# Two granules of the rotation behind each of the last three convolution steps

## The reference

```python
x = x + depthwise_conv5x5(gn(x), kernel(weight))       # each channel with its own 5x5 taps
x = x + einsum('hvc,bchw->bvhw', R, gn(x))             # for each image row h a 128x128 matrix R[h]
```

## Time and profile before

| | us |
|---|---|
| median of 3 runs | 428.61 (428.4 to 429.36) |
| the profiled execution | 428.04 |
| its span | 426.2 |
| PE busy | 407.3 (96% of the span) |
| DVE busy | 362.2 (85%) |
| ACT busy | 264.4 (62%) |
| POOL busy | 242.6 (57%) |
| bytes moved by DMA | 139.83 MB (10^6), mean 328 GB/s |

### The profile page before, as it was taken

One profiled execution on the slowest core, in us unless ns is written; L12 is line 12 of the kernel. 1 busy time (PEld: TensorE's weight loads), 2 busy tenths in 40 slices (PEclk: granted clock), 3 DMA queues, 4 the chain that ended last, 5 costly groups with the idle time before them and its releaser, 6 DMA issues.

```text
span 426.2 us, 8616 instructions
## 1 busy us (share of the span) xinstructions
PE 407.3 (96%) x3110; PEld 200.7 (47%) x3110; DVE 362.2 (85%) x691; ACT 264.4 (62%) x513; POOL 242.6 (57%) x312
## 2 busy tenths in 40 slices
PE   7899999999999999999999999999999994999992
PEld 2345555555555555544444445444444541444440
DVE  4899999999999999889998889999887783687872
ACT  2386676667656775696666777666677534477760
POOL 7588675667656765696555676555553153344440
PEclk9999999999999999999999999999999998899997
DMA  8826579599977677977899999999999999999998
GB/s 295 374 58 226 213 221 316 220 334 380 373 250 281 241 272 270 341 255 245 339 360 372 301 384 344 352 391 330 411 361 394 407 377 386 401 427 427 424 425 344
DMA packets 36955, 139.83 MB, mean 328 GB/s; under 512 B 7472, under 2 KB 7600, under 8 KB 24368
## 3 DMA queue, kind: packets, MB, share of 16 engines
q1 hardware_dynamic: 17056, 107.29, 66.5%
q10 hardware_dynamic: 19856, 31.99, 20.8%
HBM read 72.14 MB, written 67.12 MB: 327 GB/s over the span
## 4 chain that ended last, share of the span: by engine, by line
PE 89%; POOL 3%; DMA 2%; issue 2%; DVE 1%; ACT 1%; ACTq 0%; SPq 0%; POOLq 0%
PE ps L743 61%; PE ps L778 26%; POOL area L447 2%; PE ps L784 2%; DMA kept<-x_scratch 1%; DMA norm<-affine 1%; DVE area L652 1%; PE ps L753 1%; PE ps L761 0%; ACT gn L542 0%; POOL gn L470 0%; POOL area L461 0%; ACTq L261 0%; DVE tin L652 0%; ACT std L514 0%
## 5 line engine op out<-in xcount | busy, mean ns | idle before, releaser
L743 PE MATMUL ps<-area 64*64 64x496 f32 (+2 forms) x2560 | 281.6, 586 | 2.4 <-POOL area L447 2.4
L743 PEld LDWEIGHTS ps<-area 64*64 64x64 f32 x2560 | 140.3, 133 | 98.4 <-issue 86.4
L447 POOL TENSOR_TENSOR area<-mask,area 128x325 f32<-128x325 f32 x128 | 132.3, 1056 | 44.3 <-PE ps L743 33.0
L778 PE MATMUL ps<-gn,rot 128*128 128x512 f32 x256 | 117.3, 611 | 6.2 <-ACT gn L542 5.9
L521 ACT ACTIVATE area<-area,affine 128x256 f32<-128x256 f32 x192 | 97.9, 588 | 34.4 <-DVE affine L632 32.5
L534 ACT ACTIVATE area<-ps 64x512 f32<-64x512 f32 x128 | 75.6, 591 | 31.2 <-PE ps L743 28.5
L610 DVE BATCH_NORM_STATS2 stats<-area 128x6 f32<-128x512 f32 x128 | 80.6, 689 | 3.8 <-DMA area<-in_x_dram 3.8
L778 PEld LDWEIGHTS ps<-gn,rot 128*128 128x128 f32 x256 | 48.3, 194 | 72.3 <-issue 60.4
L461 POOL TENSOR_SCALAR area<-area,affine 128x256 f32<-128x256 f32 x62 | 46.1, 752 | 63.3 <-DVE affine L632 63.2
L619 DVE BATCH_NORM_STATS2 stats<-area 128x6 f32<-128x512 f32 x128 | 81.1, 697 | 1.1
L652 DVE TENSOR_TENSOR tin<-ps,tin 128x512 f32<-128x512 f32 x68 | 46.8, 691 | 15.7 <-PE ps L778 15.6
(11 more groups left out here) (26 smaller groups left out, 110.3 us busy)
## 6 DMA issues: line engine op xcount, KB each, us to landing
area<-in_x_dram SPq DMA_DIRECT2D x31, 1024.0 KB, 6.5
x_scratch<-area ACTq DMA_DIRECT2D x29, 1024.0 KB, 7.4
out_dram<-tin SPq DMA_DIRECT2D x17, 1024.0 KB, 8.9
tin<-x_scratch SPq DMA_DIRECT2D x15, 1024.0 KB, 11.4
out_dram<-area SPq DMA_DIRECT2D x10, 1024.0 KB, 13.2
area<-x_scratch SPq DMA_DIRECT2D x7, 1024.0 KB, 11.8
rot<-in_rota_dram SPq DMA_DIRECT2D x4, 1024.0 KB, 9.1
kept<-x_scratch SPq DMA_DIRECT2D x16, 256.0 KB, 10.2
```

Of the source, the lines that this page charges most:

```text
L447: last = nc.gpsimd.tensor_tensor(taps[k % TRING][:, c * KW:(c + 1) * KW].rearrange("p d (b r) -> p d b r", r=TAPS), mask[:].rearrange("p d ...
L743: last = nc.tensor.matmul(ps[half, bank + c].rearrange("p (j w) -> p j w", j=J)[:, :, outs], taps[k % TRING][rows, (2 * pair + c) * KW + d ...
L778: nc.tensor.matmul(ps[:, rot_bank(m), :], rot[:, n % UNITS * RH + h], gn[n % NRING][:, h], start=True, stop=True).then_inc(rotated, 1)
```

## The change

Behind steps 29, 30 and 31 two granules are rotated in place of one (`granules_of`): 10 and 11, 12 and 13, 14 and 15; for step 31, the first behind its matmuls as before, and granule 15 right after it with the last averages between its rows. Thirteen granules of the first half rotated by the end of step 31 and its rotation become sixteen. ACT and POOL normalise them, and DVE adds them, in the same steps.

In SP's order the loads of the loop's iterations 29, 30 and 31 stay at their places and fetch other granules (12 and 11, 14 and 13, 15, where there were 11 and 13, 12 and 14, 15). Granule 11 is stored in iteration 31 instead of 32, granules 12 and 13 in iteration 32 instead of behind the loop. Quarters 0 to 2 are loaded ahead for nine granules, 20 to 28, where there were six, 20 to 25; granules 26 to 28 were loaded whole, later. `IN_QUARTERS` goes from 10 to 13. The buffers of granules 11 to 31 are dealt out anew, and with them the waits for stored granules: 9, 10 and 11 within the loop, 12 and 13 behind it.

```diff
+TWICE = STEPS_ALL - 3
-IN_QUARTERS = 10
+IN_QUARTERS = 13
...
-        tin = [own[n % DRING] for n in range(KEPT)] + [granule_on(at_x[n]) for n in (2, 3, 4)]
+        tin = [own[n % DRING] for n in range(11)]
+        tin += [granule_on(at_x[2]), own[3], granule_on(at_x[3]), own[0], granule_on(at_x[4])]
         tin += [kept[:, n] for n in range(FRONT)]
-        tin += [own[1], granule_on(at_x[5]), own[2], granule_on(at_n[0]), granule_on(at_n[1]), granule_on(at_t),
-                granule_on(at_t + TILE), granule_on(at_x[0]), own[3], granule_on(at_x[1]), own[0], granule_on(at_x[2])]
+        tin += [own[1], own[2], granule_on(at_x[2]), own[3], granule_on(at_x[3]), granule_on(at_x[5]),
+                granule_on(at_n[0]), granule_on(at_n[1]), granule_on(at_t), granule_on(at_t + TILE),
+                granule_on(at_x[0]), granule_on(at_x[1])]
...
+        def granules_of(s):
+            if s < TWICE:
+                return range(s - START, s - START + 1)
+            first = TWICE - START + 2 * (s - TWICE)
+            return range(first, first + 2)
-        LAST_THREE = KEPT * RH - 1
+        LAST_THREE = granules_of(STEPS_ALL - 1)[0] * RH
```

In SP's loop over s:

```diff
-                    store_granule(sp, s - START - 2)
+                    for n in granules_of(s - 2):
+                        store_granule(sp, n)
...
                     store(sp, s - 2)
-                    store_granule(sp, 11)
+                    for n in granules_of(s - 2):
+                        store_granule(sp, n)
                     load_norms(1)
-                n = s - START + 1
-                if 2 <= n < KEPT:
+                if START + 1 <= s < STEPS_ALL - 1:
+                    n = granules_of(s + 1)[0]
                     if n >= DRING:
-                        sp.wait_ge(out_stored[n - DRING], 16)
+                        sp.wait_ge(out_stored[{12: 7, 14: 8}.get(n, n - DRING)], 16)
                     load_granule(sp, n)
-                n = s - 29 + KEPT
-                if KEPT <= n < UNITS:
+                if s >= TWICE and s < STEPS_ALL:
                     await_stores(sp, s - 3)
                     sp.wait_ge(stats_ready, measured(s - 3 + LAG))
-                    load_granule(sp, n)
+                    load_granule(sp, granules_of(s)[1])
...
-                    for n, left in ((20, 9), (22, 10)):
+                    for n, left in ((20, 9), (21, 10), (22, 11)):
                         sp.wait_ge(out_stored[left], 16)
```

Behind that loop, where afterwards stores 14 and 15 and loads 29 to 31 follow without a wait for a store, and granules 26 to 28 are no longer loaded whole:

```diff
             for r in range(QUARTERS - 1):
-                load_quarter(sp, 21, r)
+                load_quarter(sp, 25, r)
+            for n, left in ((23, 12), (24, 13)):
+                sp.wait_ge(out_stored[left], 16)
+                for r in range(QUARTERS - 1):
+                    load_quarter(sp, n, r)
             sp.wait_ge(convolved, 2 * STEPS_ALL)
             for r in range(QUARTERS - 1):
-                load_quarter(sp, 23, r)
+                load_quarter(sp, 26, r)
             store(sp, STEPS_ALL - 1)
-            for n in (24, 25):
+            for n in (27, 28):
                 for r in range(QUARTERS - 1):
                     load_quarter(sp, n, r)
-            store_granule(sp, 12)
             await_stores(sp, STEPS_ALL - 1)
             for n in range(UNITS, UNITS + IN_QUARTERS):
                 load_quarter(sp, n, QUARTERS - 1)
```

On ACT (POOL normalises in the same order):

```diff
+                if s > TWICE:
+                    normalise_rows(granules_of(s)[0])
                 evict(s, 0)
                 store(act, s - 1)
-                if s + 1 >= START:
+                if START <= s + 1 <= TWICE:
                     normalise_rows(s + 1 - START)
+                if s >= TWICE:
+                    normalise_rows(granules_of(s)[1])
             s = STEPS_ALL - 1
             evict(s - 1, 1)
             take_root(s + 1)
-            normalise_rows(KEPT)
+            normalise_rows(UNITS - 2)
             send_norms(act, s - 3)
             evict(s, 0)
+            normalise_rows(UNITS - 1)
             evict(s, 1)
```

On DVE, and on PE:

```diff
-                add_rows(s - START, range(RH))
+                for n in granules_of(s):
+                    add_rows(n, range(RH))
...
                 if s >= START:
-                    rotate(s - START, range(RH))
+                    for n in granules_of(s):
+                        if n < UNITS - 1:
+                            rotate(n, range(RH))
             last_round = ROUNDS - 1
-            rotate(KEPT, (0, 1))
+            rotate(UNITS - 1, (0, 1))
```

More of the change, by code:

```diff
@@ L50 @@
 START = 19
-KEPT = STEPS_ALL - START
+TWICE = STEPS_ALL - 3
 DRING = 4
@@ L379, in _ @@
                 load_quarter(sp, n, QUARTERS - 1)
[L380 to L385, removed]
             store_granule(sp, 14)
             load_granule(sp, 29)
-            sp.wait_ge(out_stored[12], 16)
+            store_granule(sp, 15)
+            sp.wait_ge(stats_ready, measured(ROUNDS - 1))
             load_granule(sp, 30)
-            store_granule(sp, 15)
-            sp.wait_ge(out_stored[13], 16)
             load_granule(sp, 31)
@@ L496, in _ @@
                     spread_taps(s + 2, (2, 3))
-                if s + 1 >= START:
+                if START <= s + 1 <= TWICE:
                     normalise_rows(s + 1 - START)
-            for n in range(KEPT, GRANULES):
+                if s == TWICE:
+                    normalise_rows(granules_of(s)[1])
+                if s > TWICE:
+                    for n in granules_of(s):
+                        normalise_rows(n)
+            for n in range(granules_of(STEPS_ALL - 1)[0], GRANULES):
                 normalise_rows(n)
@@ L577, in _ @@
             send_norms(act, s - 2)
-            normalise_rows(KEPT + 1)
             take_root(s + 3)
-            normalise_rows(KEPT + 2)
             send_norms(act, s - 1)
             send_norms(act, s)
-            for n in range(KEPT + 3, GRANULES):
+            for n in range(UNITS, GRANULES):
                 normalise_rows(n)
@@ L710, in _ @@
             measure_sum(s)
-            add_rows(KEPT - 1, (0, 1))
+            add_rows(UNITS - 2, (0, 1))
             deviate(s + 3)
-            add_rows(KEPT - 1, (2,))
+            add_rows(UNITS - 2, (2, 3))
             scale(s + 3)
-            add_rows(KEPT - 1, (3,))
-            for n in range(KEPT, GRANULES):
+            for n in range(UNITS - 1, GRANULES):
                 add_rows(n, range(RH))
@@ L819, in _ @@
                 if s >= START:
-                    rotate(s - START, range(RH))
+                    for n in granules_of(s):
+                        if n < UNITS - 1:
+                            rotate(n, range(RH))
             last_round = ROUNDS - 1
-            rotate(KEPT, (0, 1))
+            rotate(UNITS - 1, (0, 1))
             for half in (low, high):
                 average_mean(last_round, half)
-            rotate(KEPT, (2, 3))
+            rotate(UNITS - 1, (2, 3))
             for half in (low, high):
                 average_spread(last_round, half)
-            for n in range(KEPT + 1, GRANULES):
+            for n in range(UNITS, GRANULES):
                 rotate(n, range(RH))
```

## The result

The changed kernel takes 433.55 us (median of 4 runs, 432.74 to 434.56) against 428.99 for the kernel before beside it: a ratio of 1.0107, 95% interval 1.0074 to 1.0140, some 4.6 us slower. The profiled execution took 432.74 with a span of 430.9, against 428.04 and 426.2. It was forecast slower, to 436.9, with a range from 431 to 441.

The account below looks back on a forecast made before the run. PE and the DMA engines were taken as near-equal bounds at the end. Granule 16's last quarter 10.6 us later, less 2.3 from the last landing, gave +8.3 on 426.2, hence median 436.9 us, range 431 to 441.

Parts of the forecast that it names:

- last quarter: Granule 16's last quarter load, which lets PE start again: forecast to land at 367.8, 10.6 us later than 357.2.
- store of 13: Granule 13's store in SP's iteration 32: forecast to land at 353.6, with SP's later quarters and x1 store behind its wait.
- likeliest case: The forecast's main chain to the kernel's end: 436.9 us, own range 434 to 440, chance 0.70.
- lowest bound: Whole kernel at 433.7: store of 13 landing 2.6 us earlier and a last landing of 4.0 instead of 4.6.
- step 3: SP's iteration 32 begins at 340.5; stores land at 348.4, 351.0 and 353.6, SP by then free and waiting.
- lower bound for this store: Store of 13 without a queue at 340.5: landing at 351.0 rather than 353.6, kernel at 434.3.
- 58.2 of rotations: PE's gapless run over granules 16 to 31, slow clock at its start included, kept at 58.2 us after the restart.
- last half store: Final store at the kernel's end: forecast to land in 4.6 us against 6.9 before, returning 2.3 us.
- B: Rival: granule 13's normalising on ACT comes 2.6 us late, so step 31 ends later too; 439.5 us, chance 0.09.
- A: Rival: store of 13 lands by 348, x1 store out at 352, PE 5.1 us later; 431.4 us, chance 0.10.
- C: Rival, not slower: DMA engines set the end, granule 16 in time by 359.5; 426.3 us, chance 0.11.
- Signs: Expected trace: x1 store near 357 after SP waits, PE idling 16 to 17 us, DMA share falling after some 390.

Follow-up runs that it names:

- experiment 1: Changed kernel with the x1 store of step 31 issued first behind SP's loop, ahead of the waits for stores 12 and 13: 434.07 us, ratio to before 1.0125.
- experiment 3: Kernel before, no rotation moved, x1 store of step 31 issued behind the quarters of 24 and 25 and the store of granule 12: 433.11 us, ratio 1.0101.
- experiment 7: Changed kernel with quarters loaded ahead for granules 20 to 25 only, 26 to 28 loaded whole later: 434.96 us, ratio to before 1.0150.
- experiment 5: One unused 0.72 MB transfer added to the tail of both kernels: before 430.56 us, ratio 1.0043; changed 433.16 us, ratio to before 1.0113.
- experiment 2: Changed kernel, x1 store of step 31 first and last quarters of 16 to 23 ahead of the wait for store 13: 430.53 us, ratio to before 1.0044.

## Why the prediction came out right, and what in it was luck

The direction was right, and so was the path: more ahead of x1's last store in SP's order, a later last quarter, a longer idling of PE, part of it returned by the last landing. The link in its middle was not: SP hardly stands at the store of 13. The sum was too large, +8.3 against +4.7 in the profiled executions. The median of 433.55 lies in the range from 431 to 441, but under the likeliest case's own 434 to 440 and just under its lowest bound, 433.7. Three terms each err the same way by 1.2 or 1.3 us: the last quarter, the run of rotations and the last landing.

- *"SP is by then free and waits"*, in step 3, is what failed. SP waited 0.2 us for that store. The sum gave SP nothing for the three loads of norms, 4.03 us, nor for the issues beside them; in the trace it comes to the wait at 351.6, and the store lands at 351.8. That the two fall together is luck, and the forecast of x1's store came near by it. Of the 11.6 us by which the last quarter goes out later, 6.7 are the later start of iteration 32 (7.3 forecast) and 4.9 SP's longer issuing.
- *The store of 13* landed at 351.8, forecast 353.6. The queue was shorter than I counted: iteration 31 began at 323.7 and not 324.4, behind engines that stood part idle, and store 10 landed in 5.8 us, at 329.5, forecast 330.8. The x1 store went out at 355.8 (357.4), landed at 362.3 (363.5), the last quarter at 366.6 (367.8). The times kept their order, 1.2 us early. (The lower bound for this store has a slip: 5.8 and twice 2.6 from 340.5 on give 351.5 and not 351.0, and the bound's time is 434.8. And the row of DMA shares holds 19 slices of nine tenths and a last one of eight, not 18.)
- *The 58.2 of rotations* were taken over whole, with the slow clock in them. Measured 57.0. In the changed kernel the clock granted was 0.50 from the restart at 369.4 to 373.0 and 1.00 behind it:

```profile
369.40:373.00 3.60, 3.59 (x5) 1.52 (x6) 0.69 (x1) 2.42 (x5) 0.71 (x2) 0.50 0.98 380
373.00:376.00 3.00, 3.00 (x8) 1.34 (x7) 2.30 (x4) 0.99 (x2) 0.91 (x2) 1.00 1.00 418
```

  That is 3.6 us at 1.2 GHz, against 6.0 in the kernel before (from its restart at 360.0 to 366); at half speed the 2.4 us fewer are worth 1.2. PE had stood idle longer, and the clock came back sooner, but the one does not follow from the other: after 16.77 us of idling in experiment 1 the same run took 57.65 us, and over all the runs shown here it takes 56.6 to 58.2. This term's miss is chance.
- *The last half store* took 3.3 us, forecast 4.6, because I took a store as unhindered that was not: the 5.8 of 309.6, at a time when the DMA engines were full. The quarter taken as unhindered, 4.3, was not either: while SP waited in experiments 3 and 7, granule 16's last quarter landed in 3.0. The Trainium skill's rule (DMA: Bandwidth & Descriptors, Anatomy of one DMA — SWDGE (gpsimd) path) gave an estimate of 3.2, and the trace agrees with it: 3.3. I had set it aside for a row that measured something else.
- *B* did not occur: the double rotations have no gap. *A* is near in its number, 431.4, but the x1 store did not go out at 352. In experiment 1 the store was early, at 347.5, and the last quarter was not, because what stood between them had not moved. *C* named the right other bound (experiment 5). Its condition, granule 16's last quarter landed by 359.5, was missed by 7 us; experiment 2 came near it, 360.2, and its queue was not emptied: engines that are full to the end give back little for an earlier PE, 1.9 us for 6.4 there.
- *Signs:* the DMA share was to fall after some 390; it fell after 410. The sum had emptied the queue before the stores, but they join it from 375.6 on: a store landed in 15.6 us there and in 7.8 at 403.1, 1 us less from each to the next. "SP waiting for stores" before x1's store was 0.2 us. That x1's store would be the one link that decides was too simple: its place matters (experiment 3), but moving it alone returns nothing (experiment 1).

## What to carry to other kernels

A chain that ended last names what released a wait, not how long anyone stood at it: read the wait itself, and what the waiting engine did before. When two resources are both near their bound, cost an edit on each of them: what it does to the chain of the busiest engine, and how many microseconds the DMA engines go without work. A queue issued in program order, as here, needs, ahead of each wait, enough bytes to last until the wait is over; and steps made longer need more bytes in each. Before taking a row as an unhindered transfer, look at the DMA share in its stretch.

## What the runs showed of the hardware

Idle time of the DMA engines showed in the end of the kernel: 3.0 us of it in two stretches of experiment 3 with 4.1 us more span, 3.2 in experiment 7 with 2.6 us more span, although PE started 2.2 us earlier. And 0.72 MB more in a full queue cost 2.2 us in the median, with an interval from 1.2 to 2.5; 425 GB/s give 1.7. An issue took SP 0.61 us in the six quarters from 351.81 on and 1.34 in the three loads of norms, both with the engines full.
